# Attention over 512 query tiles: when TensorE weighs the values, and the order of one turned quarter between the score halves

## The reference, cut to what matters

```python
scores = jnp.einsum('bhqd,bhkd->bhqk', q / math.sqrt(HEAD_DIM), k)
scores = scores + attention_bias                 # 2 x 16 x 2048 x 2048, float32
scores = jnp.where(src_mask, -jnp.inf, scores.astype(jnp.float32))
probs = jax.nn.softmax(scores, axis=-1)
ctx = jnp.einsum('bhqk,bhkd->bhqd', probs, v)
```

## Time and profile before

| | |
|---|---|
| time, median of three | 3677.97 us |
| the profiled execution's own time | 3678.13 us |
| its span | 3676.1 us |
| PE busy | 3436.5 us, 93% |
| PEld busy | 1956.3 us, 53% |
| DVE busy | 2488.7 us, 68% |
| ACT busy | 1893.6 us, 52% |
| POOL busy | 2077.3 us, 57% |
| HBM | 763.12 MB read, 142.61 MB written |

### The profile page before, as it was taken

One profiled execution on the slowest core, in us unless ns is written; L12 is line 12 of the kernel. 1 busy time (PEld: TensorE's weight loads), 2 busy tenths in 40 slices (PEclk: granted clock), 3 DMA queues, 4 the chain that ended last, 5 costly groups with the idle time before them and its releaser, 6 DMA issues. The chain is left out here.

```text
span 3676.1 us, 61259 instructions
## 1 busy us (share of the span) xinstructions
PE 3436.5 (93%) x18338; PEld 1956.3 (53%) x18338; DVE 2488.7 (68%) x4176; ACT 1893.6 (52%) x2544; POOL 2077.3 (57%) x642
## 2 busy tenths in 40 slices
PE   6787779999999999999999999998499999999997
PEld 2333336666666666666666666665244444444443
DVE  3444449999999999999999999997333424434332
ACT  2212228888888888888888888886111111111110
POOL 0000039999999999899999899996112202201100
PEclk9898889999999999999999999999799999999999
DMA  6787789999999999999999999996612202201100
GB/s 235 231 262 249 242 311 373 349 344 347 352 394 348 352 344 351 374 367 350 343 348 350 394 348 350 349 346 218 181 42 69 69 0 68 68 19 49 46 12 12
DMA packets 291097, 906.13 MB, mean 246 GB/s; under 512 B 94208, under 2 KB 94208, under 8 KB 214272
## 3 DMA queue, kind: packets, MB, share of 16 engines
q1 hardware_dynamic: 238976, 805.14, 61.4%
q10 hardware_dynamic: 49536, 92.29, 7.3%
q0 software_dynamic: 2560, 8.39, 0.6%
HBM read 763.12 MB, written 142.61 MB: 246 GB/s over the span
## 5 line engine op out<-in xcount | busy, mean ns | idle before, releaser
L478 POOL TENSOR_TENSOR ring<-ring,penb 128x1856 f32<-128x1856 f32 x512 | 1904.0, 3756 | 629.3 <-DMA penb<-pen_scratch 543.6
L574 ACT ACTIVATE ring<-ring,low 128x2048 f32<-128x2048 f32 x512 | 1028.7, 2009 | 317.4 <-DVE low L542 317.4
L655 PEld LDWEIGHTS b_T<-ident,ring 128*128 128x128 f32 x8192 | 890.4, 141 | 429.7 <-DVE probT L526 426.6
L655 PE MATMUL b_T<-ident,ring 128*128 128x128 f32 x8192 | 1091.8, 276 | 2.6 <-DVE probT L526 2.6
L542 DVE CUSTOM_DVE_ANT_0 ring<-scores,ring 128x1024 f32<-128x1024 f32 x512 | 627.2, 1225 | 176.8 <-PE scores L621 154.8
L526 DVE COPY probT<-b_T 128x512 f32<-128x512 f32 x1024 | 702.6, 686 | 4.9 <-PE b_T L655 4.8
L542 DVE CUSTOM_DVE_ANT_0 ring<-scores,ring,low_part 128x1024 f32<-128x1024 f32 x512 | 652.8, 1275 | 0.4
L621 PE MATMUL scores<-keys,queries 128*128 (+1 forms) x2048 | 621.7, 425 | 21.0 <-DMA queries<-q_rows 16.6
L678 PE MATMUL bank_ctx<-probT,values 128*32 128x512 f32 x4096 | 544.9, 604 | 0.0
L584 ACT COPY probT<-b_T 128x512 f32<-128x512 f32 x1024 | 538.0, 575 | 3.0 <-PE b_T L655 3.0
L845 POOL TENSOR_TENSOR y_out<-rot_a,rot_b 128x512 f32<-128x512 f32 x32 | 41.6, 1299 | 785.9 <-DVE rot_b L1003 785.9
(11 more groups left out here) (101 smaller groups left out, 1940.2 us busy)
## 6 DMA issues: line engine op xcount, KB each, us to landing
ring<-in_fside_Bx16xSxS SPq DMA_DIRECT2D x512, 1024.0 KB, 7.5
keys<-k_rows SPq DMA_DIRECT2D x64, 1024.0 KB, 8.6
values<-v_heads ACTq DMA_DIRECT2D x128, 256.0 KB, 5.3
queries<-q_rows SPq DMA_DIRECT2D x128, 256.0 KB, 8.0
ctx_scratch<-ctxp ACTq DMA_DIRECT2D x128, 256.0 KB, 6.6
parts<-ctx_scratch SPq DMA_DIRECT2D x128, 256.0 KB, 4.9
k_rows<-part_hi SPq DMA_DIRECT2D x64, 256.0 KB, 2.9
k_rows<-part_lo SPq DMA_DIRECT2D x64, 256.0 KB, 2.9
```

Of the source, the lines that this page charges most:

```text
L478: nc.gpsimd.tensor_tensor(ring[:, j, 0:POOL_MASKED], ring[:, j, 0:POOL_MASKED], penb[:, j, 0:POOL_MASKED], ALU.add).then_inc(masked, 1)
L574: nc.scalar.activation(ring[:, k, :], ring[:, k, :], ACT.Exp, bias=low[:, k:k + 1], scale=-1.0, accum_out=column(sums_all, trip, k)).then_ ...
L655: last = nc.tensor.transpose(turn_bank(slot, n)[:, c * P:(c + 1) * P], ring[:, slot, at:at + P], ident[:])
```

## The change

In even steps PE weighs two quarters of a unit, and does so after all four quarters are turned; in odd steps it weighs none. In odd steps PE turns quarter 0 between the two score halves. DVE copies quarters 2 and 3 of tile i-2 one after the other behind both adds. ACT copies quarter 0 of tile i-2 ahead of the exponential and quarter 1 behind it. The wait for DVE's copy of quarter 2 of tile i-3 moves in odd steps from half 1 to half 0, since quarter 0 now comes ahead of half 1.

```diff
+        WEIGH_AFTER = 3
@@ DVE
             def step(it, j):
                 add(it, j, 0)
-                copy_quarter(it, j, 3, 3)
                 add(it, j, 1)
-                copy_quarter(it, j, 2, 2)
+                copy_quarter(it, j, 2)
+                copy_quarter(it, j, 3)
@@ ACT
+            def step(it, j):
+                copy_quarter(it, j, 0)
+                exponentials(it, j)
+                copy_quarter(it, j, 1)
...
@@ PE, free_before_turn
                     if c == 0:
                         pe.wait_ge(exp_done, t + 1)
-                    else:
+                    if c == (0 if j % 2 else 1):
                         need(pe, out_dve, t * 2 - 1)
@@ PE, turn
-                        if n == 1:
+                        if n == WEIGH_AFTER and j % 2 == 0:
                             copied_before_weigh(it, j)
@@ PE, weigh
-                return (j - 2) % QT, unit, 1 if 2 <= j < 6 else 0
+                return unit, 1 if 2 <= j < 6 else 0, 0 if j % QT == 2 else 2
...
-                for c in range(4):
-                    if live(unit, UNITS):
-                        last = nc.tensor.matmul(...)
+                unit, hh, first = weighed(it, j)
+                for n in (first, first + 1):
+                    for c in range(4):
+                        if live(unit, UNITS):
+                            last = nc.tensor.matmul(...)
@@ PE, step
                 score(it, j, 0)
-                score(it, j, 1)
-                turn(it, j, 0)
+                if j % 2:
+                    turn(it, j, 0)
+                    score(it, j, 1)
+                else:
+                    score(it, j, 1)
+                    turn(it, j, 0)
                 turn(it, j, 1)
-                weigh(it, j)
                 turn(it, j, 2)
                 turn(it, j, 3)
+                if j % 2 == 0:
+                    weigh(it, j)
```

More of the change, by code:

```diff
@@ L515, in _, with copy_quarter @@
             nc.vector.tensor_copy(identb[:], ident[:]).then_inc(identb_ready, 1)
-            def copy_quarter(it, j, n, lag):
-                t, k = it * R + j - lag, (j - lag) % R
+            def copy_quarter(it, j, n):
+                t, k = it * R + j - 2, (j - 2) % R
                 hh, q = k // QT, k % QT
@@ L564, in _, with exponentials @@
             load_values(0, 1)
-            def step(it, j):
+            def exponentials(it, j):
                 i = it * R + j
@@ L575, in step, with copy_quarter @@
                                          accum_out=column(sums_all, trip, k)).then_inc(exp_done, 1)
+            def copy_quarter(it, j, n):
+                i = it * R + j
                 if live(i - 2, NT):
@@ L578, in step @@
                     hh, q = k // QT, k % QT
[L579 to L585, removed]
+                    act.wait_ge(turned, TURNED0 + (i - 2) * 4 + n + 1)
+                    if q == 0 and n == 0:
+                        act.wait_ge(pv_done, PV0 - 1 + (it * 2 if j == 2 else it * 2 + 1))
+                    nc.scalar.copy(probT[:, hh, QR * n:QR * (n + 1), q * P:(q + 1) * P],
+                                   turn_bank(k, n)[:].rearrange("p (c q) -> p c q", c=QR)).then_inc(out_act, 1)
+            def step(it, j):
+                copy_quarter(it, j, 0)
+                exponentials(it, j)
+                copy_quarter(it, j, 1)
                 unit, hh = closing(it, j), 0 if j < QT else 1
@@ L660, in weighed @@
                 unit = it * 2 - 2 if j < 2 else it * 2 - 1 if j < 6 else it * 2
-                return (j - 2) % QT, unit, 1 if 2 <= j < 6 else 0
+                return unit, 1 if 2 <= j < 6 else 0, 0 if j % QT == 2 else 2
             def copied_before_weigh(it, j):
-                n, unit, hh = weighed(it, j)
+                unit, hh, n = weighed(it, j)
                 if live(unit, UNITS):
-                    pe.wait_ge(out_act if n < 2 else out_dve, (unit * QT + QT - 1) * 2 + n % 2 + 1)
+                    if n == 0:
+                        pe.wait_ge(v_in[hh], it * 16 if j == 2 else it * 16 + 16)
+                        need(pe, ctx_copied, unit)
+                    pe.wait_ge(out_act if n == 0 else out_dve, (unit * QT + QT) * 2)
             def weigh(it, j):
[L672 to L675, removed]
-                for c in range(4):
-                    if live(unit, UNITS):
-                        last = nc.tensor.matmul(bank_ctx[DH * c:DH * (c + 1), :], values[:, hh, QR * n + c, :],
-                                                probT[:, hh, QR * n + c, :], start=(n == 0), stop=(n == 3))
-                if live(unit, UNITS) and n == 3:
+                unit, hh, first = weighed(it, j)
+                for n in (first, first + 1):
+                    for c in range(4):
+                        if live(unit, UNITS):
+                            last = nc.tensor.matmul(bank_ctx[DH * c:DH * (c + 1), :], values[:, hh, QR * n + c, :],
+                                                    probT[:, hh, QR * n + c, :], start=(n == 0), stop=(n == 3))
+                if live(unit, UNITS) and first == 2:
                     last.then_inc(pv_done, 1)
```

## The result

The changed kernel takes 3875.84 us (median of four, 3874.55 to 3877.17) against 3677.98 for the one before: 5.4% slower, ratio 1.0539 with a 95% interval of 1.052 to 1.0557. The forecast was 3883, the range 3800 to 3960.

A forecast was written before the change was run, and what follows sets the result against it. PE's own work and the loop through DVE, tied, bound the kernel. Removed work bought 0.24 a pair, new waits cost 1.02; with the trip boundary, 512 x 0.40 = 205 us on 3678.13 gave 3883, range 3800 to 3960.

The forecast's parts named there:

- The tie: In the kernel before, PE's own work and the loop through DVE's copy of quarter 2 both set the 3.952 us step.
- What PE saves: Around the weighing, two switches become one per pair of steps: 0.24 us a pair, 0.12 a step.
- The wait for the exponential: In even steps, half 0's second score matmul waits for the odd step's exponential: 0.80 us a pair.
- The tie of the new loops: Even step's half 1: last score matmul possible at 4.265 by DVE's copy 2, at 4.295 by its slot: tied.
- The wait of quarter 2: In even steps, quarter 2's third transpose waits for ACT's copy of quarter 0: 0.22 us late.
- The unshown costs: Guessed times no row shows, such as add to add and weighing to score; half at once is 50 to 80 us.
- The sum: Whole loop: 8.69 us a pair, 4.345 a step; with the trip boundary 0.40 more a step, 205 us, giving 3883.
- PE alone: Rival: exponential and copies come in time, only the saved 0.12 a step counts; 3.83 a step, 3617 us; chance 0.08.
- the pair's clock: Times in us within one pair of steps, with 0 where the odd step starts; the exponential was put at 3.66.
- Only DVE's loop: Rival: ACT's quarter copy and exponential overlap more, only the loop through DVE binds; 4.22 a step, 3817 us; chance 0.08.
- The clock: Rival: PE's clock falls because PE stands in every pair; +118 us on the forecast, 4001 us; chance 0.05.
- Gain and stall: Rival: DVE runs ahead enough to even out short and long steps, so no change within 0.2%; chance 0.03.

The follow-up runs named there:

- Experiment 1: Kernel before with DVE's part alone: DVE copies quarters 2 and 3 of tile i-2 behind both adds; 3663.27 us, ratio 0.9959.
- 9: Kernel before with DVE's adds, the exponential, POOL's penalty and ACT's copies each over half their columns, PE's work whole; 3664.17 us, ratio 0.9958.
- 10: Changed kernel with DVE's adds, the exponential, POOL's penalty and ACT's copies each over half their columns, PE's work whole; 3606.85 us, ratio 0.9804.
- Experiments 6 to 8: Changed kernel with the exponential over half its columns (3874.68 us), with both DVE adds over half (3872.98), and with both cuts (3663.80).
- experiment 6: Changed kernel with the exponential over 1024 of its 2048 columns; 3874.68 us, ratio 1.0534.
- experiment 11: Changed kernel with PE's quarters turned earlier and DVE's and ACT's orders differing between odd and even steps; 3819.3 us, ratio 1.038.
- 12: Kernel of experiment 11 with the odd step's wait for ACT's quarter 0 copy moved from quarter 2's third transpose to quarter 3's first; 3664.25 us, ratio 0.9962.
- experiments 2 and 4: Kernel before with ACT copying quarter 0 ahead of the exponential: 3799.68 us; changed kernel with ACT's order as before, exponential first: 3971.35 us.

## Why the prediction was right

- **The tie.** The kernel before was said to be held by PE's own work and the loop through DVE's copy of quarter 2, tied. Experiment 1 loosened the loop and found PE's own work 15.5 us below, 0.03 a step. 377 waits sound like more than that; as the prediction said, PE lost only a few hundredths in each.
- **What PE saves.** 0.24 a pair was taken; 9 and 10 measure 0.224. In the pair above, sixteen weighing matmuls start at 1609.93 and the next weight load at 1611.78, 1.85 us; I had 1.82 + 0.09. The Trainium skill ("TensorE: Matmul & The Clock Gate", list of specifications) lets weight loads be pulled ahead of matmuls in flight. Taken without a limit, as in the prediction, it would leave nothing to gain by merging. 57 us between 9 and 10 say that this switch isn't covered.
- **The wait for the exponential.** 0.80 a pair predicted. The slot of that matmul was at 1605.88 + 0.11 + 0.235 = 1606.23 and it started at 1606.95 + 0.11, 0.83 late.
- **The tie of the new loops.** I had 4.265 and 4.295 for the two candidates of the last score matmul. Experiments 6 to 8 show the tie: 1, 3 and 212 us.
- **The wait of quarter 2.** 0.22 predicted. Ten transposes from 1607.85 end at 1608.94, the next starts at 1609.12 + 0.06, 0.24 late.
- **The unshown costs.** Add to add: 1.35 taken, 1.38 found (1604.08 to 1605.46). Copy to exponential: 0.47 taken, 0.48 found (1604.32 to 1604.80). Weighing to score: 0.20 taken, and the weight load comes 0.09 after the last slot (1609.93 + 1.92 − 0.16 = 1611.69), as I had. The bounds were 0.1 to 0.6 wide; that each guess came within 0.03 is partly luck.
- **The sum.** 3.15 us from the odd penalty to the even one were predicted, 3.17 are there (1604.59 to 1607.76). 4.345 a step was predicted, 4.34 found. The forecast is 7 us high: I added 0.01 a step for the trip boundary, in case the new wait didn't cover it. 512 x 0.393 is 201, the difference found is 198. The parts measured one by one agree: 1.07 of waits, less 0.22 of switches, less the 0.06 that the kernel before lost in its own loop (experiment 1), is 0.79 a pair, against 0.77 found (198 / 256).
- **The rivals.** PE alone (3617) would have needed the exponential before 2.9 on the pair's clock; it ended where it was put. Its price was 10 us high, since PE's own work in the new order is 3606.85 (experiment 10). Only DVE's loop (3817): experiment 6 leaves just that loop and stays at 3875. That price was wrong in itself, as it had dropped the wait of quarter 2, which doesn't hang on the exponential (57.5 us in 223 pairs there). The clock stayed at 1.00 through the stalls. Gain and stall didn't cancel.
- What failed was an expectation, not the forecast: in experiment 11 I had placed a wait where its reason is, and not where the code has it, and the times expected in 11 and 12 don't follow from their own 3.86 a step.

## What to carry to other kernels

When engines hand single buffers to each other step by step, uneven steps have a price: a short step gives the helpers little time, a long one gives them time that they can't use, and here the saved switch (0.22 us a pair) was dwarfed by the waits (1.07). It isn't a rule that steps must be even: the orders of experiment 12 keep the uneven weighing and end level with the best even kernel. Before reordering, write one period with the start of each instruction from the trace, and put each wait on the instruction that carries it in the code, not on the one that needs it. If a cut of one suspect gives nothing, cut the other too before acquitting either.

## What the runs showed that I had not expected

Two parts of one change can have opposite signs: ACT's order costs 121 us beside even weighing and gains 96 beside uneven weighing. The prediction names that order only as a burden; the expectations of experiments 2 and 4, written after the result, already have both signs. And a wait stands two transposes earlier than it must: in the changed kernel, with only transposes behind it, it costs 0.24 us a pair, and with a score half behind it it cost 155 us. What moving it would give in the changed kernel itself wasn't run.
